# A transformer layer on one core: the last batch's feed-forward part by token halves, and the order of the last three batches

## The chip, the cores and the metric

One core of a Trainium2 chip. The metric is the device time of one execution in microseconds (us). The times of before are those of three runs. A profiled execution has its own time, and a span: from its first to its last instruction. Engines: PE is TensorE, ACT ScalarE, DVE VectorE, POOL GpSimd, and SP issues DMAs.

## What is computed

Eight batches of 1024 tokens of width 128, fp32. Each goes through one attention head and a feed-forward part (FFN) with a layer norm behind either.

```python
q, k, v = x @ wq, x @ wk, x @ wv           # 128 x 128 weights; rotary turn on half of q and k
p = softmax(q @ k.T / 128 + causal mask)
x = layernorm(x + (p @ v) @ wo)            # over the 128 features, no gain or bias
h = gelu(x @ sign(w1).T * alpha1 + b1)     # 512 hidden
x = layernorm(x + h @ sign(w2).T * alpha2 + b2)
```

## The kernel before

Every engine has its own program: a list of small tasks in an order written out by hand, and semaphores between the lists. An engine runs its list strictly in order, so a task that waits holds all that stand behind it. Tasks are named by a number and a batch: `scores(r, c)` is row tile r (128 queries) of batch c; `(h, c)` is half h (512 tokens) of a batch. Batches are 0 to 7, written `B - 1` for 7 and `B - 2` for 6. The text below writes `up(3, 6)` for `up(3, B - 2)`.

One batch goes through these tasks. `x_squares` (DVE) turns x; `xT_high` (ACT) and `xT_low` (POOL) split it into two parts that TensorE's fast format holds. `project` (PE) makes q and k; `rotate` (DVE), `tok_copy` (ACT) and `rotation_sum` (POOL) turn them; `turn_qk` (PE), `qkT_high` (ACT), `qkT_low` (DVE) transpose and split. `scores` (PE), `row_max` (DVE), `exponentials` (ACT), `turn_row` (DVE) and `carry` (SP: 16 DMAs) lead to the transposed probabilities; rows 4 to 7 of the last batch go by `turn_row` on PE and `row_copy` on ACT and DVE instead. `weigh` and `project_out` (PE, with `pxT_copy` on ACT) give the attention output of a half, `residual1` and `statistics1` (DVE), `first_factors` (POOL) and `first_norm` (DVE) the first layer norm.

The FFN: `turn_x1` (PE), `x1T_high` (ACT), `x1T_low` (DVE); `up(j, c)` (PE) makes a quarter j of the hidden features for all 1024 tokens in a PSUM pair of banks; `gelu` and `hidden_high` (ACT) and `hidden_low` (POOL) work on 128 x 1024; `down` (PE) sums the quarters of one half of the tokens; `y_half` (ACT), `turn_y` (PE), `residual2` and `statistics2` (DVE), `second_factors` (POOL), `second_norm` (ACT), `store` (SP).

PSUM holds three pairs of banks and two single banks, given out in rotation (`next_pair`, `next_bank`). A task on PE that takes one waits until the last user of it has been read out (`wait_freed`).

In the last batch of the kernel before, gelu writes back into its PSUM pair for j > 0, and DVE does `hidden_low` for j > 0. `norm_factors` on POOL is a chain of eight small operations per half or batch, the last of them the power -0.5; the second norm has one more, a product. `second_factors` of batch c waits for `s_y`, which the last `second_norm` of batch c - 1 raises. `residual2(0, c)` waits for the `store` of batch c - 2. ACT's Exp and Gelu need a table each, and a change between them puts an ACT_TABLE_LOAD in its queue; its copies need none.

Of the kernel before, what the change touches and what calls it, by code (L numbers as in the profile page):

```python
# [12 lines left out]
LN_EPS = 1e-5  # L13
# [3 lines left out]
def attention_ffn_kernel(nc, x, wq, wk, wv, wo, w1, b1, w2, b2, cos_t, sin_t, out):  # L17
# [32 lines left out]
    with ctx:  # L50
# [123 lines left out]
        def _(sp):  # L174
# [94 lines left out]
        def _(pool):  # L269
# [50 lines left out]
            def shifts(ts, before):  # L320

                norm_factors(stat2, ln2, ts, s_ln2, before, -1.0)
                pool.wait_ge(s_ln2, before + LN_STEPS)
                pool.tensor_tensor(ln2[:, 6, ts], ln2[:, 2, ts], ln2[:, 7, ts], ALU.mult).then_inc(s_ln2, 1)  # L324

            def second_factors(c):
                pool.wait_ge(s_stat2[0], c + 1)
                pool.wait_ge(s_stat2[1], c + 1)
                if c > 0:
                    pool.wait_ge(s_y, c)  # L330
                shifts(slice(0, NT), LN2_STEPS * c)

            def second_factors_half(h, c):
                pool.wait_ge(s_stat2[h], c + 1)
                if h == 0:
                    pool.wait_ge(s_y, c)
                shifts(slice(TG * h, TG * (h + 1)), LN2_STEPS * (c + h))
# [62 lines left out]
            rotation_sum(0, B - 1)  # L400
            rotation_sum(1, B - 1)
            hidden_low(0, 3)
            hidden_low(1, 3)
            hidden_low(2, 3)
            hidden_low(3, 3)
            second_factors(2)
# [8 lines left out]
            first_factors(1, B - 2)  # L415
# [3 lines left out]
            hidden_low(3, B - 3)  # L419
            second_factors(B - 4)  # L420
            first_factors(0, B - 1)
            first_factors(1, B - 1)
# [3 lines left out]
            hidden_low(3, B - 2)  # L426
            second_factors(B - 3)
            hidden_low(0, B - 1)
            second_factors(B - 2)
            second_factors_half(0, B - 1)  # L430
            second_factors_half(1, B - 1)

        @block.tensor
        def _(pe):
# [10 lines left out]
            def wait_freed(task, i, c):  # L445
# [5 lines left out]
                if task == "up":  # L451
                    pe.wait_ge(s_gelu[i], c + 1)
                    if c == LAST and i > 0:
                        pe.wait_ge(s_hid_lo[i], c + 1)
# [146 lines left out]

            def down_quarter(j, h, c):
# [3 lines left out]
                pe.wait_ge(s_hid_lo[j], c + 1)  # L606
# [147 lines left out]
            def ending():  # L754
# [12 lines left out]
                turn_qk(2, B - 2)  # L767
                scores(0, B - 2)
                turn_y(0, 2)
                project(0, B - 1)  # L770
                down(1, 2)
                turn_qk(3, B - 2)
                project(1, B - 1)
                scores(1, B - 2)
                weigh(0, B - 3)
                weigh(1, B - 3)
                weigh(2, B - 3)
                weigh(3, B - 3)
                turn_x1(0, B - 4)
                scores(2, B - 2)  # L780
                scores(3, B - 2)
                turn_y(1, 2)
                project_out(0, B - 3)
                scores(4, B - 2)
                turn_qk(0, B - 1)
                scores(5, B - 2)
                scores(6, B - 2)
                scores(7, B - 2)
                weigh(4, B - 3)
                weigh(5, B - 3)  # L790
                weigh(6, B - 3)
                turn_x1(1, B - 4)
                weigh(7, B - 3)
                up(0, B - 4)
                project_out(1, B - 3)
                down(0, 3)
                down(1, 3)
                up(1, B - 4)
                turn_y(0, 3)
# [9 lines left out]
                scores(1, B - 1)  # L809
                weigh(3, B - 2)  # L810
                turn_y(1, 3)
                scores(2, B - 1)
                scores(3, B - 1)
                project_out(0, B - 2)
                scores(4, B - 1)
                scores(5, B - 1)
                weigh(4, B - 2)
                weigh(5, B - 2)
                weigh(6, B - 2)
                weigh(7, B - 2)  # L820
                turn_x1(0, B - 3)
                scores(6, B - 1)
                scores(7, B - 1)
                turn_x1(1, B - 3)
                down(0, B - 4)
                turn_row(4, B - 1)
                project_out(1, B - 2)
                turn_row(5, B - 1)
                down(1, B - 4)
                up(0, B - 3)  # L830
                up(1, B - 3)
                turn_y(0, B - 4)
                turn_y(1, B - 4)
                up(2, B - 3)
# [451 lines left out]
        def _(dve):  # L1286
# [667 lines left out]
```

## Time and profile before

| | |
|---|---|
| median of 3 runs | 306.39 us (305.84 to 307.79) |
| the profiled execution's own time | 308.83 us |
| its span | 307.0 us |
| granted TensorE clock, mean of the span | 0.962 of full |
| busy: PE, DVE, ACT, POOL | 87%, 75%, 76%, 57% of the span |

The span in 40 slices shows PE at nine tenths or more almost without a break from the eleventh slice to the 33rd, and thin in the last seven. Busy shares are of a whole span, so they say little about the end; the sections below go by stretches of it. In rows of the timeline the first two columns are start and length in us. Rows that stand for several instructions have "xN" and the length of the run. The length of one instruction includes its latency; instructions behind each other overlap, so the pitch (start to start) is shorter. What stands in brackets is the idle time ahead of the row and what ended it. In a row of the windows each engine has its busy time and the number of its instructions, then come the granted clock (1.00 is 2.4 GHz), the DMA share and GB/s.

### The profile page before, as it was taken

To read this page: it belongs to the slowest core of one execution; us is meant where nothing else is said; L and a number is where in the kernel's file an instruction comes from. 1 tells how busy PE (TensorE), PEld (TensorE's weight loads), DVE (VectorE), ACT (ScalarE), POOL (GpSimd) and SP (SyncE) were. 2 spreads that over 40 slices of the span, in tenths; PEclk is the share of its full clock that TensorE was granted. 3 is DMA by queue.
4 is the path that set the end of the run, shared out by engine and by line. 5 is a ranking of instruction groups with operands and counts; after the bars stand their busy time and mean duration, and the time that the engine had idled before them with its cause. 6 is when DMAs were issued, how large, how long until landed. Compare 5 with 4: busy or idle time off the path is not lost.

```text
span 307.0 us, 5699 instructions
## 1 busy us (share of the span) xinstructions
PE 267.2 (87%) x1797; PEld 234.6 (76%) x1797; DVE 230.6 (75%) x551; ACT 233.7 (76%) x385; POOL 175.8 (57%) x281
## 2 busy tenths in 40 slices
PE   0759779999998999999999999999999998959540
PEld 0649578887987898989898989898998897847320
DVE  2399999898988897799779977996696473550832
ACT  1246466555679979998899999887996996897852
POOL 1333424024366396639972884949279769796534
PEclk9969999999999999999999999999999999987985
DMA  9928286377539627652674157114932302002222
GB/s 154 226 64 147 61 135 153 80 111 163 155 74 176 158 52 112 150 136 50 108 166 126 46 138 173 24 46 123 268 83 66 88 2 72 0 0 68 63 71 74
DMA packets 62925, 31.97 MB, mean 104 GB/s; under 512 B 37808, under 2 KB 58800, under 8 KB 62896
## 3 DMA queue, kind: packets, MB, share of 16 engines
q1 hardware_dynamic: 60816, 31.35, 46.2%
q10 hardware_dynamic: 2080, 0.26, 0.6%
q8 instruction: 15, 0.25, 0.3%
q14 instruction: 14, 0.11, 0.1%
HBM read 10.23 MB, written 4.19 MB: 47 GB/s over the span
## 4 chain that ended last, share of the span: by engine, by line
PE 65%; SPq 12%; ACT 8%; DVE 4%; issue 4%; DMA 3%; POOL 2%; ACTq 0%; POOLq 0%; DVEq 0%
PE bank L530 17%; PE pair L510 12%; SPq L212 10%; PE bank L590 4%; PE pair L559 4%; PE bank L591 4%; PE pair L560 4%; PE bank L541 4%; DMA xq<-in_L_attn_x_dram 3%; PE bank L582 3%; ACT res L964 2%; PE pair L572 2%; PE bank L617 2%; PE bank L548 2%; PE pair L574 2%
## 5 line engine op out<-in xcount | busy, mean ns | idle before, releaser
L343 POOL TENSOR_TENSOR hid_lo<-hid,hid_hi 128x1024 fp32r<-128x1024 f32 x29 | 68.5, 2380 | 34.4 <-ACT hid_hi L949 34.4
L530 PE MATMUL bank<-probT,xa 128*128 128x128 f32 x576 | 68.6, 276 | 0.2 <-DMA probT<-turned 0.2
L530 PEld LDWEIGHTS bank<-probT,xa 128*128 128x128 f32 x576 | 66.4, 192 | 0.9 <-DMA probT<-turned 0.3
L902 ACT ACTIVATE prob<-pair,negmax 128x128 f32<-128x128 f32 (+3 forms) x64 | 47.3, 740 | 12.6 <-DVE negmax L1331 10.8
L1331 DVE TENSOR_REDUCE negmax<-pair 128x1 f32<-128x128 f32 (+3 forms) x64 | 47.2, 743 | 6.5 <-PE pair L513 6.3
L1341 DVE STREAM_TRANSPOSE turned<-prob 128x128 f32<-128x128 f32 (+7 forms) x60 | 43.0, 739 | 1.0 <-DMA probT<-turned 1.0
L510 PE MATMUL pair<-qkT_hi 128*128 128x512 f32 (+2 forms) x96 | 37.9, 395 | 3.3 <-ACT tok L916 2.0
L941 ACT ACTIVATE hid<-pair,b_sb,alpha 128x1024 f32<-128x1024 f32 x29 | 34.2, 1203 | 0.8 <-PE pair L560 0.6
L510 PE MATMUL pair<-qkT_hi,qkT_lo 128*128 128x512 f32 (+2 forms) x96 | 33.5, 349 | 0.0
L510 PE MATMUL pair<-qkT_lo,qkT_hi 128*128 128x512 f32 (+2 forms) x96 | 33.4, 348 | 0.0
L313 POOL TENSOR_TENSOR tok<-rot_cos,rot_sin 128x512 f32<-128x512 f32 x16 | 21.1, 1322 | 20.5 <-ACT tok L916 20.5
L964 ACT ACTIVATE res<-res,ln 128x128 f32<-128x128 f32 x60 | 25.9, 489 | 7.7 <-POOL ln L324 7.7
L307 POOL TENSOR_TENSOR xT_lo<-xT,xT_hi 128x512 fp32r<-128x512 f32 x16 | 20.5, 1284 | 19.5 <-ACT xT_hi L909 19.5
L301 POOL TENSOR_TENSOR ln<-ln,minus_half 128x4 f32<-128x4 f32 (+1 forms) x25 | 30.3, 1213 | 2.0
L559 PE MATMUL pair<-x1T_hi,sgn1T 128*128 128x512 f32 x64 | 28.5, 445 | 2.7 <-issue 1.9
L949 ACT ACTIVATE hid_hi<-hid 128x1024 fp32r<-128x1024 f32 x29 | 30.4, 1058 | 0.1
L289 POOL TENSOR_TENSOR ln<-stat 128x4 f32<-128x4 f32 (+1 forms) x25 | 5.1, 206 | 43.7 <-DVE stat L1364 37.6
L1452 DVE TENSOR_TENSOR qkT_lo<-bank,qkT_hi 128x512 fp32r<-128x512 f32 x32 | 21.6, 680 | 8.6 <-ACT qkT_hi L930 8.3
L916 ACT ACTIVATE tok<-pair 128x1024 f32<-128x1024 f32 x16 | 16.4, 1024 | 14.3 <-DVE rot_sin L1447 14.3
L560 PE MATMUL pair<-x1T_lo,sgn1T 128*128 128x512 f32 x64 | 26.9, 420 | 0.0
L1359 DVE SCALAR_TENSOR_TENSOR res<-bank,rinv,xa 128x128 f32<-128x128 f32 x64 | 18.3, 342 | 9.2 <-issue 9.1
L582 PE MATMUL bank<-ident,tok 128*128 128x128 f32 x128 | 20.0, 286 | 5.0 <-DVE qkT_lo L1452 2.7
(97 smaller groups left out, 631.1 us busy)
## 6 DMA issues: line engine op xcount, KB each, us to landing
probT<-turned SPq DMA_DIRECT2D x112, 104.0 KB, 2.2
probT<-turned SPq DMA_DIRECT2D x128, 40.0 KB, 1.9
xa<-in_L_attn_x_dram SPq DMA_DIRECT2D x8, 512.0 KB, 4.5
xq<-in_L_attn_x_dram SPq DMA_DIRECT2D x30, 128.0 KB, 3.8
out_dram<-res SPq DMA_DIRECT2D x7, 512.0 KB, 3.5
cos_sb<-in_cos_dram SPq DMA_DIRECT2D x1, 512.0 KB, 4.5
sin_sb<-in_sin_dram SPq DMA_DIRECT2D x1, 512.0 KB, 6.0
hid<-in_L_ffn_w_dram SPq DMA_DIRECT2D x2, 256.0 KB, 5.2
```

The source lines that it names most:

```text
L212: sp.dma_start(probT[g][k * BLK:(k + 1) * BLK, n, :, :], turned[g][n * BLK:(n + 1) * BLK, k, :, :]).then_inc(s_probT_in[g], 16)
L343: pool.tensor_tensor(hid_lo[:, j, :], hid[:, j, :], hid_hi[:, j, :].bitcast(F32), ALU.subtract).then_inc(s_hid_lo[j], 1)
L510: ins = pe.matmul(dst[:, lo:hi], qp[:, 0, me], kp[:, 1, lo:hi], start=n == 0, stop=n == 2 and not diagonal)
L530: ins = pe.matmul(bank_of["px", r // TG, c][:, me], xa[c % 2][:, j, :], probT[g][:, :, spot + j, :], start=j == 0, stop=j == r)
L559: pe.matmul(dst[:, half(h)], sgn1T[:, j, :], x1T_hi[:, half(h)], start=True, stop=False)
L560: ins = pe.matmul(dst[:, half(h)], sgn1T[:, j, :], x1T_lo[:, half(h)], start=False, stop=True)
L902: act.activation(prob[r % 3][:, 0:(r + 1) * P], pair_of["score", r, c][:, 0:(r + 1) * P], ACT.Exp, bias=negmax[:, r:r + 1], accum_out=rows ...
L941: act.activation(dst, pair_of["up", j, c][:, :], ACT.Gelu, bias=b1_sb[:, j:j + 1], scale=alpha1[:, j:j + 1]).then_inc(s_gelu[j], 1)
L949: act.activation(hid_hi[:, j, :], src, ACT.Copy).then_inc(s_hid_hi[j], 1)
L964: ins = act.activation(res2[c % 2][:, t, :], res2[c % 2][:, t, :], ACT.Identity, bias=ln2[:, 6, t:t + 1], scale=ln2[:, 7, t:t + 1])
L1331: dve.tensor_reduce(negmax[:, r:r + 1], pair_of["score", r, c][:, 0:(r + 1) * P], axis=AX.X, op=ALU.max, negate=True).then_inc(s_max[r], 1)
L1341: dve.transpose(turned[g][:, :, spot:spot + r + 1, :].rearrange("p k m j -> p m k j"), prob[r % 3][:, 0:(r + 1) * P].rearrange("p (m k j) ...
```

## The change

1. Last batch, FFN by halves of the tokens. `up_half(h, q, 7)` makes two quarters of the hidden features for one half in a pair. `gelu_half` works in PSUM (128 x 512, in place) on ACT; `hidden_high_half` is on ACT for j = 0, 2, 3 and on DVE for j = 1; all `hidden_low_half` are on DVE, reading PSUM. `down_quarter` takes all four quarters of the first half and then those of the second.
2. Last batch, both norms: DVE makes mean and variance (`bn_aggr`) and two small operations (`first_means`, `second_means`), POOL the power (and for the second norm the product).
3. All five lists have a new order from about `turn_qk(2, 6)` on. Among the moves: on PE the FFN of batch 5 and its `project_out(1, 6)` stand ahead of `scores(5..7, 7)`, and `up(0..3, 6)` among `weigh(4..7, 7)`; on ACT `gelu(0..3, 5)` ahead of `exponentials(5..7, 7)`; on SP `tokens(6)` ahead of `carry(0, 6)`, and `carry(1, 6)` ahead of `tokens(7)`.

```diff
 # SP
             carry(1, B - 3)
+            tokens(B - 2)
             carry(0, B - 2)
             store(1)
-            tokens(B - 2)
+            carry(1, B - 2)
             tokens(B - 1)
-            carry(1, B - 2)
             carry(0, B - 1)
...
 # POOL
+            def first_rstd(h, c):
+                ts = slice(TG * h, TG * (h + 1))
+                pool.wait_ge(s_ln1[h], LN_STEPS * c + 3)
+                pool.tensor_tensor(ln1[:, 7, ts], ln1[:, 5, ts], minus_half[:, ts], ALU.pow).then_inc(s_ln1[h], 1)
+
+            def second_rstd(h, c):
+                ts = slice(TG * h, TG * (h + 1))
+                before = LN2_STEPS * c + 5 * h
+                pool.wait_ge(s_ln2, before + 3)
+                pool.tensor_tensor(ln2[:, 7, ts], ln2[:, 5, ts], minus_half[:, ts], ALU.pow).then_inc(s_ln2, 1)
+                pool.wait_ge(s_ln2, before + 4)
+                pool.tensor_tensor(ln2[:, 6, ts], ln2[:, 4, ts], ln2[:, 7, ts], ALU.mult).then_inc(s_ln2, 1)
...
             second_factors(B - 4)
-            first_factors(0, B - 1)
-            first_factors(1, B - 1)
+            first_rstd(0, B - 1)
             hidden_low(0, B - 2)
             hidden_low(1, B - 2)
             hidden_low(2, B - 2)
             hidden_low(3, B - 2)
+            first_rstd(1, B - 1)
             second_factors(B - 3)
-            hidden_low(0, B - 1)
             second_factors(B - 2)
-            second_factors_half(0, B - 1)
-            second_factors_half(1, B - 1)
+            second_rstd(0, B - 1)
+            second_rstd(1, B - 1)
 # PE
+            def up_half(h, q, c):
+                pe.wait_ge(s_x1T_lo[h], c + 1)
+                dst = next_pair("up_half", 2 * h + q, c)
+                for k in range(2):
+                    j = 2 * q + k
+                    pe.matmul(dst[:, half(k)], sgn1T[:, j, :], x1T_hi[:, half(h)], start=True, stop=False)
+                    ins = pe.matmul(dst[:, half(k)], sgn1T[:, j, :], x1T_lo[:, half(h)], start=False, stop=True)
+                ins.then_inc(s_up[2 * h + q], 1)
...
+                weigh(6, B - 1)
+                up(3, B - 2)
                 weigh(7, B - 1)
-                project_out(0, B - 1)
+                turn_x1(0, B - 1)
                 project_out(1, B - 1)
-                turn_x1(0, B - 2)
...
+                up_half(0, 0, B - 1)
+                up_half(0, 1, B - 1)
                 turn_y(1, B - 3)
...
                 down(0, B - 2)
                 down(1, B - 2)
+                turn_x1(1, B - 1)
                 turn_y(0, B - 2)
                 turn_y(1, B - 2)
+                up_half(1, 0, B - 1)
+                up_half(1, 1, B - 1)
                 down_quarter(0, 0, B - 1)
+                down_quarter(1, 0, B - 1)
+                down_quarter(2, 0, B - 1)
+                down_quarter(3, 0, B - 1)
                 down_quarter(0, 1, B - 1)
-                down_quarter(1, 0, B - 1)
                 down_quarter(1, 1, B - 1)
-                down_quarter(2, 0, B - 1)
                 down_quarter(2, 1, B - 1)
-                down_quarter(3, 0, B - 1)
                 turn_y(0, B - 1)
                 down_quarter(3, 1, B - 1)
                 turn_y(1, B - 1)
 # ACT
+            def gelu_half(h, j, c):
+                act.wait_ge(s_up[2 * h + j // 2], c + 1)
+                mine = pair_of["up_half", 2 * h + j // 2, c][:, half(j % 2)]
+                act.activation(mine, mine, ACT.Gelu, bias=b1_sb[:, j:j + 1], scale=alpha1[:, j:j + 1]
+                               ).then_inc(s_gelu[j], 1)
...
 # DVE
+            def means(stat, ln, h, done, before):
+                ts = slice(TG * h, TG * (h + 1))
+                for t in tiles(h):
+                    ins = dve.bn_aggr(ln[:, 2:4, t], stat[:, t, :])
+                ins.then_inc(done, 1)
+                dve.wait_ge(done, before + 1)
+                dve.tensor_scalar(ln[:, 4, ts], ln[:, 2, ts], -1.0, None, ALU.mult).then_inc(done, 1)
+                dve.tensor_scalar(ln[:, 5, ts], ln[:, 3, ts], LN_EPS, None, ALU.add).then_inc(done, 1)
...
```

The new end of ACT's list, from `hidden_high(3, 6)` on: `second_norm(0..6, 4)`, `gelu_half(0, 0)`, `(0, 1)`, `(0, 2)`, `second_norm(7, 4)`, `y_half(0, 6)`, `gelu_half(0, 3)`, `hidden_high_half(0, 0)`, `x1T_high(1, 7)`, `y_half(1, 6)`, `hidden_high_half(0, 2)`, `(0, 3)`, `second_norm(0..4, 5)`, `gelu_half(1, 0)`, `second_norm(5..7, 5)`, `gelu_half(1, 1)`, `hidden_high_half(1, 0)`, `gelu_half(1, 2)`, `(1, 3)`, `hidden_high_half(1, 2)`, `(1, 3)`, `y_half(0, 7)`, `second_norm(0..3, 6)`, `y_half(1, 7)`, `second_norm(4..7, 6)`, `second_norm(0, 1, 4, 5; 7)`.

The new end of DVE's list, from `first_norm(0..3, 7)` on: `x1T_low(0, 7)`, `residual1` and `statistics1` of tiles 4 to 7, `first_means(1, 7)`, `residual2(1, 5)`, `statistics2(1, 5)`, `first_norm(4..7, 7)`, `x1T_low(1, 7)`, `hidden_high_half(0, 1)`, `residual2(0, 6)`, `residual2(1, 6)`, `hidden_low_half(0, 0)`, `(0, 1)`, `statistics2(0, 6)`, `(1, 6)`, `hidden_low_half(0, 2)`, `(0, 3)`, `hidden_high_half(1, 1)`, `hidden_low_half(1, 0..3)`, `residual2(0, 7)`, `statistics2(0, 7)`, `residual2(1, 7)`, `second_means(0, 7)`, `statistics2(1, 7)`, `second_means(1, 7)`, `second_norm(2, 3, 6, 7; 7)`.

## Rows read from the trace of the kernel before

**Rows 1.** Windows: 184.5 to 258.5, to 281.6, to the end, all engines.

```profile
184.50:258.50 74.00, 74.00 (x538) 66.98 (x536) 53.21 (x147) 64.90 (x109) 51.53 (x79) 1.00 0.36 90
258.50:281.60 23.10, 18.51 (x77) 14.48 (x77) 10.57 (x35) 19.58 (x26) 19.59 (x34) 0.85 0.16 46
281.60:307.00 25.40, 10.20 (x45) 6.70 (x43) 11.79 (x28) 14.12 (x28) 11.12 (x30) 0.81 0.22 63
```

**Rows 2.** Timeline of PE, 255 us to the end.

```profile
271.58 0.66 PE L548 MATMUL bank<-ident,x 128*128 128x128 f32 x4 [1.60 <-DVE x L1373]
274.08 0.77 PE L559 MATMUL pair<-x1T_hi,sgn1T 128*128 128x512 f32 x1 [1.85 <-issue]
...
297.53 1.08 PE L617 MATMUL bank<-ident,yT 128*128 128x128 f32 x4 [1.50 <-ACT yT L955]
```

**Rows 3.** The chain that ended last, from 200 us: PE's pieces at their pitch.

```profile
216.94 0.44 PE bank L582 x4
...
256.64 1.85 PE bank L541 x16
...
264.93 0.23 PE pair L559
...
274.85 0.43 PE pair L560
```

**Rows 4.** Timeline of ACT, from 187 us.

```profile
187.87 1.28 ACT L902 ACT_TABLE_LOAD   x1
189.16 0.37 ACT L902 ACTIVATE prob<-pair,negmax 128x128 f32<-128x128 f32 x1
...
260.60 0.60 ACT L934 ACTIVATE x1T_hi<-bank 128x512 fp32r<-128x512 f32 x1 [0.44 <-PE bank L548]
...
268.11 2.28 ACT L941 ACTIVATE hid<-pair,b_sb,alpha 128x1024 f32<-128x1024 f32 x2
...
286.24 2.79 ACT L964 ACTIVATE res<-res,ln 128x128 f32<-128x128 f32 x7
...
294.03 0.76 ACT L955 ACTIVATE yT<-bank,b_sb,alpha 128x512 f32<-128x512 f32 x1
...
303.39 0.88 ACT L964 ACTIVATE res<-res,ln 128x128 f32<-128x128 f32 x2 [2.25 <-POOL ln L324]
```

**Rows 5.** Timeline of DVE, from 252 us.

```profile
252.60 0.23 DVE L1350 RECIPROCAL rinv<-rowsum 128x4 f32<-128x4 f32 x2
257.63 2.16 DVE L1359 SCALAR_TENSOR_TENSOR res<-bank,rinv,xa 128x128 f32<-128x128 f32 x8 [4.80 <-issue]
...
270.33 1.19 DVE L1373 TENSOR_SCALAR x<-res,ln 128x128 f32<-128x128 f32 x4
...
273.29 0.69 DVE L1409 TENSOR_TENSOR x1T_lo<-bank,x1T_hi 128x512 fp32r<-128x512 f32 x1 [0.74 <-ACT x1T_hi L934]
...
289.97 2.36 DVE L1396 TENSOR_TENSOR hid_lo<-pair,hid_hi 128x1024 fp32r<-128x1024 f32 x2 [0.20 <-ACT hid_hi L949]
...
296.33 0.87 DVE L1425 BATCH_NORM_STATS2 stat<-res 128x6 f32<-128x128 f32 x4
```

**Rows 6.** Timeline of POOL, from 271 us.

```profile
271.42 7.02 POOL L343 TENSOR_TENSOR hid_lo<-hid,hid_hi 128x1024 fp32r<-128x1024 f32 x3 [0.75 <-ACT hid_hi L949]
278.39 0.21 POOL L289 TENSOR_TENSOR ln<-stat 128x8 f32<-128x8 f32 x1
...
281.82 0.20 POOL L324 TENSOR_TENSOR ln<-ln 128x8 f32<-128x8 f32 x1
...
297.28 0.21 POOL L289 TENSOR_TENSOR ln<-stat 128x4 f32<-128x4 f32 x1 [4.45 <-DVE stat L1425]
...
298.92 1.04 POOL L301 TENSOR_TENSOR ln<-ln,minus_half 128x4 f32<-128x4 f32 x1
```

**Rows 7.** SP's timeline, and DMA issues with KB and median us to landing.

```profile
181.13 30.06 SPq L212 DMA_DIRECT2D probT<-turned  x32
...
out_dram<-res SPq DMA_DIRECT2D x7, 512.0 KB, 3.5
```

More of the change, by code:

```diff
@@ L452, in wait_freed @@
                     pe.wait_ge(s_gelu[i], c + 1)
-                    if c == LAST and i > 0:
-                        pe.wait_ge(s_hid_lo[i], c + 1)
+                if task == "up_half":
+                    h, q = divmod(i, 2)
+                    for j in (2 * q, 2 * q + 1):
+                        pe.wait_ge(s_hid_lo[j], c + 1 + h)
                 if task == "rowT":
@@ L803, in ending @@
                 up(3, B - 4)
+                down(1, 3)
+                turn_y(0, 3)
                 scores(0, B - 1)
-                turn_qk(3, B - 1)
+                scores(1, B - 1)
+                turn_y(1, 3)
+                scores(2, B - 1)
                 weigh(0, B - 2)
@@ L1748, in _ @@
             residual1(7, B - 4)
-            qkT_low(2, B - 2)
-            residual2(0, 2)
-            first_norm(0, B - 4)
             statistics1(4, B - 4)
@@ L1760, in _ @@
-            statistics1(7, B - 4)
+            turn_row(0, B - 2)
             rotate(1, B - 1)
-            reciprocals(1, B - 3)
-            qkT_low(3, B - 2)
-            row_max(1, B - 2)
-            turn_row(0, B - 2)
+            residual2(1, 2)
             statistics2(0, 2)
-            x1T_low(0, B - 4)
-            row_max(2, B - 2)
-            residual2(1, 2)
-            turn_row(1, B - 2)
+            row_max(3, B - 2)
+            first_norm(4, B - 4)
             residual1(0, B - 3)
@@ L1772, in _ @@
             residual1(1, B - 3)
-            row_max(3, B - 2)
-            row_max(4, B - 2)
-            statistics1(0, B - 3)
+            residual1(2, B - 3)
+            first_norm(5, B - 4)
+            turn_row(1, B - 2)
+            first_norm(6, B - 4)
+            first_norm(7, B - 4)
+            residual1(3, B - 3)
+            x1T_low(0, B - 4)
             turn_row(2, B - 2)
             turn_row(3, B - 2)
+            row_max(4, B - 2)
+            x1T_low(1, B - 4)
+            statistics1(0, B - 3)
@@ L1778, in _ @@
+            turn_row(4, B - 2)
+            statistics2(1, 2)
+            statistics1(1, B - 3)
             row_max(5, B - 2)
-            residual1(2, B - 3)
-            residual1(3, B - 3)
             row_max(6, B - 2)
-            first_norm(4, B - 4)
-            turn_row(4, B - 2)
-            statistics1(1, B - 3)
             statistics1(2, B - 3)
-            reciprocals(0, B - 2)
-            first_norm(5, B - 4)
-            first_norm(6, B - 4)
-            first_norm(7, B - 4)
+            row_max(7, B - 2)
@@ L1790, in _ @@
+            turn_row(5, B - 2)
             statistics1(3, B - 3)
+            turn_row(6, B - 2)
             qkT_low(0, B - 1)
-            statistics2(1, 2)
-            turn_row(5, B - 2)
-            x1T_low(1, B - 4)
-            row_max(7, B - 2)
-            turn_row(6, B - 2)
+            turn_row(7, B - 2)
             residual1(4, B - 3)
@@ L1858, in _ @@
             first_norm(3, B - 2)
-            residual2(1, B - 4)
+            statistics1(7, B - 2)
+            residual1(0, B - 1)
+            residual1(1, B - 1)
+            residual1(2, B - 1)
+            residual1(3, B - 1)
+            statistics1(0, B - 1)
+            statistics1(1, B - 1)
+            statistics2(1, B - 4)
             first_norm(4, B - 2)
@@ L1892, in _ @@
             first_norm(3, B - 1)
+            x1T_low(0, B - 1)
+            residual1(4, B - 1)
+            statistics1(4, B - 1)
+            residual1(5, B - 1)
+            residual1(6, B - 1)
+            residual1(7, B - 1)
+            statistics1(5, B - 1)
+            statistics1(6, B - 1)
+            statistics1(7, B - 1)
+            first_means(1, B - 1)
             residual2(1, B - 3)
-            statistics2(0, B - 3)
             statistics2(1, B - 3)
```

425 lines of the change are left out of this document (217 added, 208 removed).

## The prediction

> **What bounds the kernel now.** I read the page's 40 slices first, then the windows around the end, then PE's timeline and the chain, and last the lists of ACT, DVE and POOL beside it. The windows show two regimes. From 184.5, where the new order begins, to 258.5 PE is busy for all of 74.00 us at full clock, with ACT at 64.90 and the others lower [rows 1]: PE's work is the bound. At 258.5 it has just finished `project_out(1, 7)`. From there PE holds 18.51 of 23.10 us and then 10.20 of 25.40, at a granted clock of 0.85 and 0.81 [rows 1]: latency is the bound. What the reader is to see is how little PE work that second regime has. At full clock a 512-column matmul has a pitch of 0.23, a group of four transposes 0.44 and a `project_out` half of 1.85, so 0.93 [rows 3]. Behind 258.5 stand, per FFN batch, 16 of `up` and 16 of `down` (7.5 us) and four groups of transposes (1.8 us); two batches lack all, batch 5 its `down` and `turn_y` (4.6 us). Sum: 2 x 9.2 + 4.6 = 23.0 us. PE could be through at 281.6; it ends at 298.6 [rows 2]. Those 17 us are pauses of 1.60 and 1.85 us and more, and a stretch at half clock, where the pitch is 0.43 [rows 2, 3]. Behind them come the last norm and the store.
>
> **The new order up to the last `weigh`.** I set out each engine's new list from 184.5, gave every task its pitch from the rows, and moved a task back wherever a wait of it ended later. On PE the same sum as above puts the end of all its work at 281.6, and 15.2 us of it stand behind `weigh(7, 7)`: `turn_x1(0, 7)` 0.44, `project_out` 0.93, four `up_half` 3.7, `down(·, 6)` 3.7, `turn_y(1, 5)` and `turn_x1(1, 7)` 0.9, `turn_y(·, 6)` 0.9, eight quarters 3.7, `turn_y(·, 7)` 0.9. So `weigh(7, 7)` can end at 266.4. Against this stand the waits. ACT is close behind: it changes between Exp and Gelu twice more than before (gelu of batch 5 is put inside the exponentials of batch 7), at 1.28 us a load [rows 4], 2.6 us together, and in my walk it hardly rests from 233 us on. I find PE held for about 0.4 us, by `y_half(0, 5)` at 253 and `x1T_low(1, 6)` at 256.7, and margins of only 0.1 to 0.5 us at `turn_qk(2, 7)`, `scores(7, 7)` (waits for `gelu(3, 5)`), `turn_row(4, 7)` (for `exponentials(5, 7)`) and `down(0, 5)` (for POOL's fourth `hidden_low`, 2.3 us each [rows 6]). DVE is held from 233 to 241 by `residual1(4, 6)`, since `project_out(1, 6)` now comes late; queued behind it are `row_max(5..7, 7)`, but their scores are later still, so it costs nothing while PE is full. SP: `tokens(6)` waits for a residual of about 184 and costs `carry(0, 6)` nothing; `carry(0, 7)` is issued from 230 to 240 and is needed at 245 (two carries, 32 DMAs, take SP 30.06 us [rows 7], of which some 10 a carry is issue and the rest waiting for turned rows). I take `weigh(7, 7)` to end at 266.7.
>
> The Trainium skill, ScalarE: Activation LUTs, section What ACT_TABLE_LOAD costs, adds a drain of about 1.4 us to every load; by it the two new changes would take 5.3 us of ACT and the end would come 2.7 us later than below. The trace does not agree: an Exp starts 1.29 us after the start of the load ahead of it, 187.87 to 189.16 [rows 4].
>
> **From the last `weigh` to the last norm.** Prices: 512-wide copy on ACT 0.60, `y_half` 0.76, `second_norm` 0.385 each (2.79 for seven) [rows 4]; 512-wide DVE step out of PSUM 0.69 (pitch 0.60, half of 2.36 / 2 fits), statistics 0.87 for four, `first_norm` 1.19 for four, `residual1` 2.16 for eight [rows 5]. `gelu_half` is not in the trace: between 0.57 (a quarter of 2.28 [rows 4]) and `y_half`'s 0.76; I take 0.65, pitch. `bn_aggr` is not either: its nearest rows are a 128 x 4 reciprocal, 0.23 for two, and the statistics, 0.87 for four [rows 5]; with two small operations and one wait I bound `means` by 0.5 and 1.3 us and take 0.9, for it resembles the small one in elements. It replaces POOL's 1.64 us of small steps (297.28 to 298.92 [rows 6]). The power stays at 1.04.
>
> The walk: `pxT_copy` and `project_out` to 268.3; DVE's residuals and statistics of the second half (queued behind `x1T_low(0, 7)`, 268.6) to 270.6, means to 271.5; POOL has four `hidden_low` of batch 6 first and makes the power to 272.6; `residual2` and `statistics2` of batch 5, then `first_norm` to 274.1. PE meanwhile makes `up_half(0, ·)` and `down(·, 6)` to 274.8, `turn_x1(1, 7)` to 275.2. ACT and DVE split it to 276.8. `turn_y(0, 6)` needs the bank that `y_half(1, 6)` empties, 276.8; `up_half(1, 0)` ends at 278.8. `residual2(0, 6)` waits for `store(4)`, which is released by `second_norm(7, 4)` at 274.0, now behind three `gelu_half`, and lands 3.5 us after its issue [rows 7], near 278. Behind this wait on DVE are the two `residual2`, then `hidden_low_half(0, 0)` and `(0, 1)`, to 280.5, and the pair for `up_half(1, 1)` comes free only then: 281.7. ACT has `second_norm` of batch 5 and the second half's gelu and copies to 285.0, DVE the second half's `hidden_low_half` to 286.3. `y_half(0, 7)` to 285.8, `turn_y(0, 7)`, last quarter to 287.0. ACT is then in `second_norm(0..3, 6)`, which POOL's factors (3.6 us, 278.39 to 282.02 in the old trace [rows 6], here from 282.1) release at 285.7, so `y_half(1, 7)` ends at 288.1, `residual2(1, 7)` at 289.5. `second_means(0, 7)` waits for `second_norm(7, 6)`, 289.6; statistics and second means to 292.3; power and product 1.3; four norms 0.88: 294.5. I add 0.05 us for each of some 25 hand-overs, 1.3 us (a first matmul after a wait takes longer than its pitch, 0.77 against 0.43 [rows 2, 3]): 295.8. In the old trace the last norms end at 304.27 (303.39 + 0.88 [rows 4]) and the span 2.7 us later, which is the last store. New span 298.5, 8.5 less than 307.0. The profiled execution's own time was 2.4 us above the median of the runs; I take the same 8.5 off the median: 306.4 - 8.5 = 298 (297.9).
>
> Work that is priced at nothing: POOL's lost `hidden_low(0, 7)` (2.3 us, it was waited for at 288.9 but POOL is no longer on the path there), and DVE's eight smaller steps for it (of the 23.1 us to 281.6 DVE fills 10.57 [rows 1], which hides most of them; the cover is gone from 280 on, and there they are counted).
>
> **Rivals.** (a) The clock. In before it was at half from 274.08 on, after the two pauses of 1.60 and 1.85 us [rows 2]; a mean of 0.85 over 23.1 us is some 7 us of it [rows 1]. The new walk has pauses of 1.6 us at 275.2 and of 1.7 at 278.8. If the clock falls there, eight matmuls of `up_half` (0.2 us each), two `turn_y` (0.44 each) and the end's share of 0.9 add 3.4 us: 301.3. For it: two pauses as long as those. Against: from 281.6 to the end PE paused for 15.2 of 25.4 us, and the mean grant was still 0.81 [rows 1]. The Trainium skill, TensorE: Matmul & The Clock Gate, section What's actually happening, says that the throttled state is the default and activity lifts it; by that the fuller PE of 258 to 275 keeps its clock, and the trace agrees so far that all of 184.5 to 258.5 ran at 1.00. (b) The narrow margins ahead of 266.7 do not hold. ACT is nearly full there, so a delay of it goes on to everything: each margin missed costs 0.5 to 1.5 us, four or five of them 3 to 6: 301 to 304. (c) The pauses are only moved: the tail's 17 us turn up before the last `weigh`, as DVE's order (`residual1(4, 6)` ahead of `row_max(5..7, 7)`, 8 us of standing still) starves ACT of exponentials. All 8 us would be lost, time 306; against it, the scores it would hold are computed after. (d) Slower: the clock falls at the first pause behind `weigh(7, 7)` and is not lifted again. PE's 15.2 us then cost 0.43 / 0.23 as much, 13 us more, time 311. It decides from about three quarters of that stretch at half clock. In before half clock lasted some 7 us and ended under steady work. (e) The halves do nothing: the end hangs on ACT's backlog of `second_norm(·, 6)`, and the whole gain is the order's. The time is then that of the forecast, within 1.5 us.
>
> **How the numbers follow.** Forecast, with (e) in it: 298, own range 295.5 to 300.5, chance 0.56. (a) 0.17; (b) 0.16; (c) 0.06; (d) 0.05. The low end of the range: both means at 0.5 (0.8 us), `store(4)` not waited for (0.7), no added hand-over time (1.3), 3 us together: 295. The high end takes in (a) and all but the worst of (b): 304. One per cent of 306.4 is 3.1 us, about what a measurement tells from no change: faster is below 303.3. From the cases: faster 0.84 (forecast, (a), two thirds of (b)), same 0.10, slower 0.06.
>
> **What would show it.** PE full and at clock 1.00 to about 266 with `weigh(7, 7)` (last L530-like matmuls) ending there and not at 256.6; two more table loads of 1.28 us on ACT; ACT's busy share above 90% from 235 to 285; `residual2(0, 6)` released by a DMA; `bn_aggr` at 0.06 to 0.2 us; last power starting less than 1 us behind the last statistics. It is wrong if PE has pauses of over 1 us before 266, or if the second half's gelu starts after 283.

## The result and the profile after

The changed kernel takes 299.12 us (median of 4 runs, 297.07 to 299.45), the kernel before 306.78 on the same chip (4 runs, 305.84 to 307.79): ratio 0.9727, 95% interval 0.9693 to 0.9761. The profiled execution took 299.45, its span is 296.6. The spans of the two profiles differ by 10.4 us, the medians by 7.7. The profiled execution of before was 2 us above its median, so what is read below as the difference between the two profiles is 2 to 3 us too large over the whole span, and the verdicts of the experiments rest on ratios of times.

Windows of after, over the first two stretches of [rows 1] and then to its end:

```profile
184.50:258.50 74.00, 73.91 (x516) 66.16 (x515) 55.95 (x156) 69.44 (x115) 54.22 (x84) 1.00 0.38 95
258.50:281.60 23.10, 19.86 (x119) 16.39 (x117) 13.72 (x49) 22.66 (x39) 14.85 (x18) 1.00 0.08 23
281.60:296.60 15.00, 4.64 (x20) 2.59 (x20) 8.86 (x32) 8.78 (x19) 5.13 (x10) 0.76 0.35 105
```

PE is as full as before up to 258.5. Behind it PE is busy for 24.5 us where it was 28.7 [rows 1], though its work is nearly the same: most of that is the half clock which is gone (0.85 before, 1.00 now, in the middle stretch). Its idle time fell from 19.8 to 13.6. ACT went from 64.90 to 69.44 and from 19.58 to 22.66 of 23.10: it is the second full engine.

PE's timeline of after: the end of `weigh(7, 7)`, and every pause of over half a microsecond behind it. [rows 2] has three pauses of before.

```profile
264.00 1.95 PE L536 MATMUL bank<-probT,xa 128*128 128x128 f32 x16
...
276.19 1.06 PE L633 MATMUL bank<-ident,yT 128*128 128x128 f32 x8 [1.61 <-ACT yT L981]
...
279.49 0.47 PE L614 MATMUL pair<-x1T_hi,sgn1T 128*128 128x512 f32 x1 [1.29 <-DVE hid_lo L1429]
...
283.43 0.47 PE L623 MATMUL bank<-hid_hi,sgn2T 128*128 128x512 f32 x1 [0.56 <-DVE hid_lo L1429]
...
287.23 0.63 PE L633 MATMUL bank<-ident,yT 128*128 128x128 f32 x4 [1.06 <-ACT yT L981]
```

Before's longest pause is not in [rows 2]. It is needed below, for the clock: behind it PE ran on at 1.00 (the windows of 287 to 289 and of 289 to 291 us, and the pitch is 0.23).

```profile
288.91 0.47 PE L607 MATMUL bank<-hid_hi,sgn2T 128*128 128x512 f32 x1 [2.75 <-POOL hid_lo L343]
289.22 0.39 PE L608 MATMUL bank<-hid_lo,sgn2T 128*128 128x512 f32 x1
289.45 0.40 PE L607 MATMUL bank<-hid_hi,sgn2T 128*128 128x512 f32 x1
```

ACT's timeline of after. The first row lies ahead of the new order and serves as a fixed point: from there to the start of the last norms it is 113.67 us.

```profile
179.25 1.28 ACT L956 ACT_TABLE_LOAD   x1
...
270.60 2.07 ACT L968 ACTIVATE pair<-pair,b_sb,alpha 128x512 f32<-128x512 f32 x3
...
284.09 0.79 ACT L981 ACTIVATE yT<-bank,b_sb,alpha 128x512 f32<-128x512 f32 x1
...
286.30 0.79 ACT L981 ACTIVATE yT<-bank,b_sb,alpha 128x512 f32<-128x512 f32 x1
...
290.77 0.88 ACT L990 ACTIVATE res<-res,ln 128x128 f32<-128x128 f32 x2 [2.14 <-POOL ln L342]
292.92 0.88 ACT L990 ACTIVATE res<-res,ln 128x128 f32<-128x128 f32 x2 [1.27 <-POOL ln L342]
```

DVE's and POOL's timelines of after. Read the first DVE row with the first POOL row: DVE's four `first_norm` of the half (0, 7) end at 260.38, and POOL starts `hidden_low` of batch 6 at 260.25, under the last of them.

```profile
259.30 1.08 DVE L1406 TENSOR_SCALAR x<-res,ln 128x128 f32<-128x128 f32 x4
...
276.86 1.29 DVE L1474 TENSOR_TENSOR res<-bank,x 128x512 f32<-128x512 f32 x2 [0.16 <-PE bank L633]
...
288.71 0.38 DVE L1436 BATCH_NORM_AGGREGATE ln<-stat 128x2 f32<-128x6 f32 x4
...
290.84 0.38 DVE L1436 BATCH_NORM_AGGREGATE ln<-stat 128x2 f32<-128x6 f32 x4 [0.69 <-POOL ln L342]
```

```profile
260.25 7.02 POOL L348 TENSOR_TENSOR hid_lo<-hid,hid_hi 128x1024 fp32r<-128x1024 f32 x3 [1.10 <-ACT hid_hi L963]
...
289.45 1.01 POOL L340 TENSOR_TENSOR ln<-ln,minus_half 128x4 f32<-128x4 f32 x1 [4.79 <-DVE ln L1440]
```

### The profile page after: what moved, and what is told of

The parts are those of the page before. It is cut to its first block, busy times and chain, and to the rows that moved or that the text cites. A ratio compares the mean times of both kernels' runs of the same rounds, so it can differ in the third digit from the quotient of the medians.

```text
span 296.6 us, 5713 instructions
## 1 busy us (share of the span) xinstructions
PE 264.4 (89%) x1797; PEld 233.4 (79%) x1797; DVE 235.0 (79%) x581; ACT 236.4 (80%) x394; POOL 167.8 (57%) x252
## 4 chain that ended last, share of the span: by engine, by line
PE 74%; ACT 11%; DVE 7%; issue 2%; DMA 2%; POOL 1%; SPq 0%; ACTq 0%; POOLq 0%; DVEq 0%
PE bank L536 21%; PE pair L516 17%; PE bank L547 5%; PE bank L588 4%; PE bank L596 4%; PE pair L565 4%; PE bank L597 4%; PE pair L566 4%; ACT res L990 3%; PE bank L554 2%; PE pair L578 2%; PE pair L580 2%; PE pair L579 2%; DMA xq<-in_L_attn_x_dram 2%; PE bank L633 2%
## 5 line engine op out<-in xcount | busy, mean ns | idle before, releaser
L348 POOL TENSOR_TENSOR hid_lo<-hid,hid_hi 128x1024 fp32r<-128x1024 f32 x28 | 66.3, 2383 | 31.3 <-ACT hid_hi L963 31.2
L516 PE MATMUL pair<-qkT_hi 128*128 128x512 f32 (+2 forms) x96 | 38.6, 402 | 2.9 <-ACT tok L932 1.9
L956 ACT ACTIVATE hid<-pair,b_sb,alpha 128x1024 f32<-128x1024 f32 x28 | 32.9, 1203 | 0.1
L963 ACT ACTIVATE hid_hi<-hid 128x1024 fp32r<-128x1024 f32 x28 | 29.3, 1057 | 0.5 <-PE bank L597 0.4
L301 POOL TENSOR_TENSOR ln<-ln,minus_half 128x4 f32<-128x4 f32 (+1 forms) x21 | 26.2, 1247 | 1.6
L289 POOL TENSOR_TENSOR ln<-stat 128x4 f32<-128x4 f32 (+1 forms) x21 | 4.4, 208 | 39.3 <-DVE stat L1397 29.7
L565 PE MATMUL pair<-x1T_hi,sgn1T 128*128 128x512 f32 x56 | 23.6, 421 | 0.9 <-ACT prob L918 0.9
L946 ACT ACTIVATE qkT_hi<-bank 128x512 fp32r<-128x512 f32 x32 | 18.7, 596 | 6.4 <-PE bank L588 6.4
```

What stands on the lines that cost most here:

```text
L301: pool.tensor_tensor(rstd, part, minus_half[:, ts], ALU.pow).then_inc(done, 1)
L348: pool.tensor_tensor(hid_lo[:, j, :], hid[:, j, :], hid_hi[:, j, :].bitcast(F32), ALU.subtract).then_inc(s_hid_lo[j], 1)
L516: ins = pe.matmul(dst[:, lo:hi], qp[:, 0, me], kp[:, 1, lo:hi], start=n == 0, stop=n == 2 and not diagonal)
L565: pe.matmul(dst[:, half(h)], sgn1T[:, j, :], x1T_hi[:, half(h)], start=True, stop=False)
L956: act.activation(hid[:, j, :], pair_of["up", j, c][:, :], ACT.Gelu, bias=b1_sb[:, j:j + 1], scale=alpha1[:, j:j + 1]).then_inc(s_gelu[j], 1)
L963: act.activation(hid_hi[:, j, :], hid[:, j, :], ACT.Copy).then_inc(s_hid_hi[j], 1)
```

## The experiments

Twelve kernels on three chips, e1 to e4, e5 to e8 and e9 to e12. Each ratio is to the kernel before on the same chip (medians there: 307.32, 308.14 and 308.46 us). After was not run again beside them, so a comparison with it assumes that a ratio carries over from chip to chip. Where a difference of two ratios is also given in us, it is that share of 306.8. The last column is the stretch from the fixed point to the start of the last norms, in the one execution that was profiled; in before it is 123.56, in after 113.67.

In three profiles this stretch has something that no edit made: the table load near 233 us comes 53.10 or 53.11 us behind the fixed point in after and in seven of the others that have the new order, but 54.01 in e1 and e9 and 53.51 in e2, ahead of all that those edits change. PE's timeline of e9 shows what it was waiting for, a DMA of the probabilities (e1 has the same wait of 0.71, e2 one of 0.22, and the other profiles with the new order none):

```profile
226.66 2.72 PE L536 MATMUL bank<-probT,xa 128*128 128x128 f32 x22 [0.71 <-DMA probT<-turned]
```

So 0.9 us of the stretches of e1 and e9 and 0.4 of e2's are not the edit's.

| | kernel | median, us | ratio, interval | stretch |
|---|---|---|---|---|
| | after | 299.12 | 0.9727 (0.9693 to 0.9761) | 113.67 |
| e1 | after without the means | 302.91 | 0.9863 (0.9834 to 0.9892) | 119.83 |
| e2 | after without the halves | 306.26 | 0.9973 (0.9953 to 0.9993) | 121.43 |
| e3 | order alone | 310.32 | 1.0108 (1.0080 to 1.0136) | 124.55 |
| e4 | before and the means | 306.16 | 0.9968 (0.9948 to 0.9988) | 121.46 |
| e5 | e1, POOL held back | 302.95 | 0.9827 (0.9790 to 0.9864) | 117.63 |
| e6 | e2, PE's pause filled | 303.82 | 0.9873 (0.9840 to 0.9906) | 118.34 |
| e7 | halves and means, old order | 306.40 | 0.9937 (0.9907 to 0.9966) | 121.19 |
| e8 | after, ACT + 2.1 us | 301.75 | 0.9788 (0.9750 to 0.9826) | 115.73 |
| e9 | after, PE + 1.87 us | 300.67 | 0.9744 (0.9711 to 0.9776) | 116.09 |
| e10 | after, own tile for `ln2` | 298.09 | 0.9669 (0.9637 to 0.9701) | 112.43 |
| e11 | after, 8 norms to DVE | 305.56 | 0.9896 (0.9862 to 0.9930) | 119.91 |
| e12 | e10 and e11 | 303.61 | 0.9838 (0.9803 to 0.9872) | 118.53 |

**e1: the means taken back.**

```diff
-            first_rstd(0, B - 1)
+            first_factors(0, B - 1)
...
-            second_rstd(0, B - 1)
+            second_factors_half(0, B - 1)
# DVE: first_means and second_means of both halves left out
```

> The changed kernel (299.1) with both norms of its last batch made on GpSimd as before; halves and order stay. Theory A, each part acts on the path: GpSimd's small steps take 1.64 us against some 0.73 that VectorE's means measured, and in the second norm the second half's chain of 3 us queues behind the first half's, so the last norms start 1.8 us later; with up to 0.9 us from the first norm: 300.9 to 301.8. Rival B, the means only fill time that ACT's backlog costs anyway: 299.1 to 299.6.

The ratio is 1.4% above after's, 4.2 us of 306.8: more than either theory gave the means. The stretch is 6.2 longer, 5.3 without that DMA wait; the execution that was profiled is the slowest of the six. The end gives its share: POOL's chain of two halves stands on the path, one row of 0.20 to 1.04 us after the other from 293.30 to 299.14, where after has a power of 1.01 and a product. From the end of the last statistics to the last norms it is 5.14 us, in after 2.78: 2.4 us. The rest comes from a place that neither theory had named. Timelines of DVE, POOL and PE in e1:

```profile
261.86 7.29 DVE L1418 TENSOR_SCALAR x<-res,ln 128x128 f32<-128x128 f32 x4 [1.47 <-POOL ln L301]
```

```profile
261.80 7.01 POOL L360 TENSOR_TENSOR hid_lo<-hid,hid_hi 128x1024 fp32r<-128x1024 f32 x3
```

```profile
269.20 0.66 PE L566 MATMUL bank<-ident,x 128*128 128x128 f32 x4 [2.25 <-DVE x L1418]
```

Four `first_norm` steps take 7.29 us instead of 1.08. With POOL's eight small steps in place of one power DVE's norms wait 1.47 us for them and then meet POOL's `hidden_low`. Three of the four lasted about as long as one POOL operation (2412 ns at most), the fourth 334 ns (the median of all 64 in the kernel is 340). POOL's own three run at their usual length. PE then waits 2.25 us, and `up_half(0, 0)` starts at half clock. The Trainium skill, SBUF — State Buffer, section Who interferes with whom, has a rule for it: VectorE and GpSimd share one pair of ports, and an instruction that takes it locks the other engine out until it ends. The rows agree.

**e5: e1 with POOL held back until `first_norm(3, 7)` is done.**

```diff
+            pool.wait_ge(s_x1[0], B)
             hidden_low(0, B - 2)
```

> e1 (GpSimd makes both norms of the last batch, 302.9) with one wait more: GpSimd starts hidden_low(0, 6) only when first_norm(0..3, 7) is through. In e1 the four first_norm took 7.29 us, as long as GpSimd's three hidden_low beside them (7.01), against 1.08 in the changed kernel, and TensorE's turn_x1(0, 7) came 3.4 us later. Theory A, VectorE's tensor_scalar and GpSimd's tensor_tensor on SBUF can't run side by side: the four take 1.1 us again, turn_x1(0, 7) follows at once and the end comes 1 to 3 us sooner: 300 to 302. Rival B, the long first_norm has another cause, or the second half sets the end anyway: 302.9 or, with GpSimd 1 us later, 303.5.

```profile
261.65 1.12 DVE L1419 TENSOR_SCALAR x<-res,ln 128x128 f32<-128x128 f32 x4 [1.46 <-POOL ln L301]
```

```profile
262.85 9.38 POOL L360 TENSOR_TENSOR hid_lo<-hid,hid_hi 128x1024 fp32r<-128x1024 f32 x4 [1.23 <-DVE x L1419]
272.19 0.21 POOL L289 TENSOR_TENSOR ln<-stat 128x4 f32<-128x4 f32 x1
```

DVE's timeline has the norms back at 1.12 us, so the collision is shown to be what made them long. The time hardly follows: 0.9827 to e1's 0.9863 is 1.1 us, with intervals that overlap, the low edge of theory A at best. POOL, now later, starts the factors of the second half at 272.19, `first_norm(4, 7)` waits for them, and half clock comes in `up_half(1, ·)` instead, 279.80 to 283.6.

**e2 and e6: the FFN by whole quarters, then with PE's pause filled.**

```diff
-                up_half(0, 0, B - 1)
-                up_half(0, 1, B - 1)
...
+                up(0, B - 1)
+                up(1, B - 1)
+                up(2, B - 1)
+                up(3, B - 1)
# gelu, hidden_high and hidden_low as in before
# e6, ahead of the first down_quarter, all overwritten by it:
+                    for _ in range(16):
+                        pe.matmul(dst[:, :], sgn1T[:, 0, :], x1T_hi[:, half(0)], start=True, stop=True)
```

> The changed kernel with the last batch's FFN made by whole quarters of all 1024 tokens as before (its up stands where the second half's stood, GpSimd has hidden_low(0) again); means and order stay. Theory A: up of 3.7 us can only begin with the second half's x1T at 277, and gelu, copies and differences of twice the width follow it; my walk has the last norms 2 us later: 301 to 302. Rival B (case e of the prediction), the end hangs on ACT's backlog of second norms and the halves do nothing: within 0.5 of 299.1. Rival C, the halves are most of the gain: 304 or more.

> e2 (whole FFN, 306.3) with 16 matmuls of 512 columns more, whose result is overwritten, put in TensorE's 4.5 us pause ahead of down_quarter(0, 0). In e2 the seven quarters behind that pause ran at a pitch of 0.43 (285.97 to 291.65). Theory A, the clock falls for the pause and that costs the end 2 to 3 us: quarters at 0.23, 303.3 to 304.5. Rival B, the clock is low there for another reason, or ACT sets the end: 306 to 307.

PE's timeline of e2, then of e6:

```profile
285.97 0.76 PE L626 MATMUL bank<-hid_hi,sgn2T 128*128 128x512 f32 x1 [4.50 <-POOL hid_lo L348]
286.53 0.63 PE L627 MATMUL bank<-hid_lo,sgn2T 128*128 128x512 f32 x1
286.96 0.63 PE L626 MATMUL bank<-hid_hi,sgn2T 128*128 128x512 f32 x1
```

```profile
279.17 3.90 PE L627 MATMUL bank<-x1T_hi,sgn1T 128*128 128x512 f32 x16
283.79 0.50 PE L629 MATMUL bank<-hid_hi,sgn2T 128*128 128x512 f32 x1 [0.73 <-POOL hid_lo L348]
284.13 0.40 PE L630 MATMUL bank<-hid_lo,sgn2T 128*128 128x512 f32 x1
284.36 0.40 PE L629 MATMUL bank<-hid_hi,sgn2T 128*128 128x512 f32 x1
```

Without the halves 2.5% are lost (7.5 us), nearly the whole gain: rival C. A quarter for all 1024 tokens has a copy of 1.04 us and, for the first quarter, POOL's 2.34 us between gelu and `down`, and PE stands still for 4.50 us. Behind that its pitch is 0.43, half clock, through seven of the eight quarters. e6 keeps PE at work through the pause; the pitch is 0.23 and 1.0% (3.1 us) comes back, as its theory A has it. So of the 7.5 us that the halves are worth some 3 are clock, and the remaining 4.4 are put down to the shorter latency; no run takes those apart.

**e3, e4, e7: the parts alone.** e3 is after with the edits of e1 and e2; e4 is before with the means; e7 is before's order with halves and means:

```diff
# e7, PE: before's list, with
-                up(0..3, B - 1)
+                up_half(0, 0, B - 1)
+                up_half(0, 1, B - 1)
+                up_half(1, 0, B - 1)
+                up_half(1, 1, B - 1)
# and gelu_half, hidden_*_half and means in the places of what they replace
```

> The changed kernel with both other parts undone: only the new order of the five lists is left. Theory A, the parts add up: 303 to 304, so the order is worth 3 to 4 of the 7.7 us. Rival B, the order is all of it: 299 to 300. Rival C, the order only pays with the halves: 306 or more.

> The kernel before (306.8) with the means alone: VectorE makes mean and variance of the last batch's two norms, GpSimd the powers; order and whole FFN stay. Theory A: the second norm's last chain is on the path there too (GpSimd's steps from 300.33 to 302.04 after the statistics at 300.25), 1 to 1.8 us less: 305 to 305.8. Rival B: nothing, 306.8.

> The old order of all five lists with both other parts of the change: the last batch's FFN by halves (up_half(0, .), down(., 6), up_half(1, .), quarters by halves, ACT's and VectorE's list ends as in the changed kernel) and the means. The order alone was 3 us slower than before (e3). Theory A, the order pays only under the halves: down(., 6) ends 6 to 7 us later here than in the changed kernel, and what follows it is the same: 304 to 306. Rival B, the order costs as much here as alone: 295 to 297. Rival C, it does nothing: 299.

The order alone costs 1.1% (3.3 us), rival C: it moves batch 7's latency chain to where POOL is in `hidden_low` (its DVE row is 7.29 us again, at 262.07) and leaves whole quarters at the end. The means alone bring 0.3% (1.0 us, the low edge of theory A), halves and means without the order 0.6% (theory A); these two intervals overlap, so halves alone are not shown to help there. With all three it is 2.7%. Given the other two, the order is worth 2.1%, the halves 2.5%, the means 1.4%: 6.0% together, more than twice the gain. The traces show one reason: the order brings `first_norm` next to POOL's `hidden_low`, and the means keep the two apart (e1, e5). Why halves and order need each other is argued and was not taken apart.

**e8 and e9: which engine binds up to 266.**

```diff
# e8, ACT, ahead of exponentials(5, 7)
+            for n in range(2):
+                act.wait_ge(s_spare, n)
+                act.activation(spare[:, :], cos_sb..., ACT.Copy).then_inc(s_spare, 1)   # 128 x 1024
# e9, PE, up(2, 5) and up(3, 5)
-                for h in range(NG):
+                for h in range(NG) if c != B - 3 or j < 2 else (0, 1, 0, 1):
```

> The changed kernel (299.1) with two copies of 128 x 1024 more on ACT (2.1 us, into a spare tile that nothing reads) ahead of exponentials(5, 7) at about 233 us. Theory A, ACT is as full as TensorE from there on (1 to 1.3 us idle to 266): the end comes 1 to 2 us later, 300 to 301.2. Rival B, only TensorE sets the pace ahead of 266: at most 0.3 us.

> The changed kernel with the first product of batch 5's last two quarters made twice: eight more 512-column matmuls, at 0.23 us each 1.87 us of TensorE ahead of scores(5,7), into the same bank with the same accumulate flags order (hid of these quarters is not the reference's). Theory A (TensorE is a bound of the stretch to 266 as much as ScalarE is; e8 showed 2.1 us of ScalarE work costing 1.9): everything from there is later by 1 to 1.9 us, ratio to the kernel before 0.979 to 0.982, about 300.3 us. Rival B (only ScalarE bounds, TensorE has slack between its waits for it): at most 0.5 us, ratio 0.973 to 0.975.

(In e9 the second pair of products starts its sums anew, so `hid` is unchanged, other than the expectation says.) e8: 2.1 us of ACT cost 0.6%, 1.9 us, and 2.06 in the stretch: ACT binds. e9's two measures disagree. By the ratio PE's 1.87 us cost 0.5 us, rival B; in the profile the stretch is 2.42 longer, of which 0.91 is the DMA wait and 1.5 the edit's, theory A. ACT shows where it enters:

```profile
179.81 1.28 ACT L956 ACT_TABLE_LOAD   x1
...
233.82 1.28 ACT L956 ACT_TABLE_LOAD   x1
...
259.55 1.28 ACT L956 ACT_TABLE_LOAD   x1
...
295.90 0.88 ACT L990 ACTIVATE res<-res,ln 128x128 f32<-128x128 f32 x2 [1.27 <-POOL ln L342]
```

The load of 259.55 is 79.74 behind the fixed point, in after it is 77.33 (256.58): 2.41, and at the load of 233.82, ahead of the added matmuls, it was 0.91 already. On the same chip e9 is 2.6 us slower than e10, whose gain over after is 1.2 to 1.8, which leaves 0.8 to 1.4. So the profile says that PE binds too; by the ratio e9 can't be told from after (0.9711 to 0.9776 against 0.9693 to 0.9761), and whether the 1.87 us cost 0.5 or 1.5 stays open.

**e10: the last batch's second-norm statistics in a tile of their own.**

```diff
+        ln2z = sb("ln2z", [P, LN_STEPS, NT])
...
-                if h == 0:
-                    dve.wait_ge(s_y, c)
...
-                means(stat2, ln2, h, s_ln2, before)
+                means(stat2, ln2z, h, s_ln2, before)
...
-            residual2(1, B - 1)
             second_means(0, B - 1)
+            residual2(1, B - 1)
```

> The changed kernel with a tile of its own for the last batch's second-norm statistics, so that the first half's means need not wait for second_norm(7,6), and with those means ahead of residual2(1,7) on VectorE. In the changed kernel's trace that half's means start at 288.71, when ScalarE's norm ends, and the second half's means wait for GpSimd's first half (0.69 us), so the last norms start at 292.92. Theory A: the first half's powers start near 286.5 and end before the second half's means are ready, so the end is earlier by 0.9 to 1.5 us: ratio 0.968 to 0.970, about 297.9 us. Rival B: ScalarE's first four norms of the last batch take over as the thing that ends last (each 0.44 us, after the norms of batch 6), or residual2(1,7) is late behind the means: less than 0.4 us, ratio 0.972 to 0.973.

ACT's timeline of e10, and DVE's:

```profile
179.93 1.28 ACT L957 ACT_TABLE_LOAD   x1
...
290.14 0.88 ACT L991 ACTIVATE res<-res,ln2z 128x128 f32<-128x128 f32 x2 [0.80 <-POOL ln2z L343]
292.36 0.88 ACT L991 ACTIVATE res<-res,ln2z 128x128 f32<-128x128 f32 x2 [1.34 <-POOL ln2z L343]
```

```profile
287.17 0.87 DVE L1482 BATCH_NORM_STATS2 stat<-res 128x6 f32<-128x128 f32 x4
288.08 0.38 DVE L1437 BATCH_NORM_AGGREGATE ln2z<-stat 128x2 f32<-128x6 f32 x4
```

Theory A holds for the end: the stretch is 1.24 shorter. The means now start right behind the statistics, where in after they stood 1.4 us longer; the first power comes 1.3 us earlier and not the 2.9 that the expectation gave it. 0.9669 is the best ratio of all. Against the kernel before it is clear of the noise; against after it is 0.6% with intervals that overlap a little, so the profile's 1.24 us is the better evidence.

**e11 and e12: batch 4's second norms to DVE.**

```diff
# ACT
-            second_norm(0..7, B - 4)
# DVE, behind first_norm(3, 7); e12 has the edits of e10 as well
+            second_norm_all(B - 4)
```

> The changed kernel with batch 4's eight second_norms taken from ScalarE (some 3.1 us near 266 to 270) and made by VectorE behind first_norm(3,7), beside GpSimd's three hidden_low runs of 260.25 to 267.27. Theory A (each of VectorE's tensor_scalar steps can be held for as long as one GpSimd instruction lasts, as e1 showed where four of them took 7.29 us instead of 1.1): eight of them take 5 us or more, x1T_low(0,7) and with it up_half(0,7) come later, and the relief of ScalarE is lost: no gain or a loss, 299 to 302 us, ratio 0.973 to 0.983. Rival B (the steps take 0.27 to 0.35 us each, 2.5 us in the 6.7 us in which VectorE waits for x1T_high(0,7) in any case): ScalarE is free 3 us sooner, and pxT(1,7) and the gelu halves follow: 296.5 to 297.5, ratio 0.965 to 0.968.

> The two edits of e10 and e11 in one kernel. If each does what its own theory gives, the time is e11's less 0.9 to 1.5 us: 297.5 to 301 with a held VectorE, 295 to 296.5 with a free one. If the end is set by ScalarE's norms of batch 6 alone, the two overlap and the sum is no better than the better of them by more than 0.5 us.

```profile
262.37 10.36 DVE L1452 TENSOR_SCALAR res<-res,ln 128x128 f32<-128x128 f32 x8
272.65 0.68 DVE L1466 TENSOR_TENSOR x1T_lo<-bank,x1T_hi 128x512 fp32r<-128x512 f32 x1
```

```profile
262.31 7.03 POOL L348 TENSOR_TENSOR hid_lo<-hid,hid_hi 128x1024 fp32r<-128x1024 f32 x3 [1.09 <-ACT hid_hi L963]
270.15 2.50 POOL L348 TENSOR_TENSOR hid_lo<-hid,hid_hi 128x1024 fp32r<-128x1024 f32 x1 [0.81 <-ACT hid_hi L963]
```

```profile
273.38 0.80 PE L614 MATMUL pair<-x1T_hi,sgn1T 128*128 128x512 f32 x1 [3.47 <-DVE x1T_lo L1466]
```

The three timelines of e11 (DVE, POOL, PE) are e1's collision made on purpose: eight steps in 10.36 us, POOL hardly disturbed, PE idle for 3.47 and then at half clock. The loss of 1.7% (5.2 us) is larger than theory A's 3 us at most; the theory had left out the clock, and how much of the loss is the clock's no run tells. e12 is 0.6% below e11, as e10 is below after: the two edits add.

## Why the prediction was right, and where it was not

The total was 298.0, the time 299.12. Its steps against the profile of after:

| step | predicted | seen |
|---|---|---|
| `weigh(7, 7)` ends | 266.7 | 265.8 (264.00 + 1.95, with latency) |
| `up_half(1, 0)` ends (next start) | 278.8 | 278.0 (277.81 + the pitch) |
| `up_half(1, 1)` starts, ends | 280.5, 281.7 | 279.49, 280.50 |
| `y_half(0, 7)`, `y_half(1, 7)` end | 285.8, 288.1 | 284.88, 287.09 |
| `second_means(0, 7)` starts | 289.6 | 288.71 |
| last norms end | 295.8 | 293.80 |
| span | 298.5 | 296.6 |

Up to `second_means(0, 7)` each step is 0.8 to 1.2 us early, and 0.6 of that was there ahead of 184.5 already: the fixed point stands at 179.25, in before at 179.83. The last norms are 2.0 early, for one reason: the walk itself ended them at 294.5, and the prediction added 1.3 us for hand-overs on top. The trace shows no room for this term, and it is the largest error of the sum. What the profile gave beyond the forecast the median took back: the forecast subtracted 8.5 from the median, and 7.7 were measured. The walk's span is 1.9 us too long and the total 1.1 too short; that the two errors nearly cancel is luck.

**Right.** PE full and at 1.00 to the last `weigh`, ACT behind it (busy 9.57 or more of each 10 us from 230 to 280), two more table loads at 1.28. `residual1(4, 6)` held DVE for 8.3 us ahead of 240.15 and cost nothing. `gelu_half` has a pitch of 0.67 (three take 2.07, one 0.72; 0.65 taken). `second_means(0, 7)` waits for `second_norm(7, 6)`, and e10 shows that this wait and the order behind it cost 1.2 us. `bn_aggr` is 0.09 a tile, inside its sign of 0.06 to 0.2.

**Rival (a), the clock, did not come**, though the pauses did: 1.61 and 1.29 us, and the clock stayed at 1.00 to the end of PE's work. Its price of 3.4 us was not tested; e6 puts half clock over fourteen matmuls of e2's end at some 3 us. The prediction's argument for it, "two pauses as long as those", went by the length of a pause, and the length of one does not decide: in e5 one of 1.14 and one of 1.45 us were followed by half clock, in after one of 1.61 was not, and nor was the 2.75 of before, which its own trace had. What does decide is not shown here.

**Terms that were off.** `store(4)` was not waited for: its issue was at 273.11, and `residual2(0, 6)` at 276.86 was released by PE, where the prediction named a DMA as a sign. It cost little: `hidden_low_half(0, 1)` ends at 279.34, where the walk has 280.5, and the walk is about 0.9 late all along. `means` takes 0.66 (288.71 to the power at 289.45 is 0.74 with the hand-over), not 0.9. The second half's means wait 0.69 us for POOL's product of the first half, a wait that the walk did not have. By it a second sign fails: the last power starts 1.43 us behind the last statistics (290.14 to 291.57) and not less than 1.

**What did not hold is (e)**, which the forecast counted in: "The halves do nothing", and the whole gain is the order's. e3 has the order alone at 3.3 us slower, e2 has the halves at 7.5 us. The mechanism that (e) named, ACT's backlog of `second_norm(·, 6)`, exists, as the wait ahead of `second_means(0, 7)`; but e10 prices it at 1.2 us, and it does not make the halves worthless. The walk's sum had all three parts in it and so came out right; the credit for each did not.

**What the prediction missed** is DVE against POOL. It costed `first_norm` at 1.19 wherever it stood. In after it is 1.08, but narrowly: the last of the four is under way when POOL starts at 260.25. The prediction had no term for this, so that it came out is luck. That the means on DVE shorten POOL's chain ahead of this point, and so keep the two apart, is part of why they are worth 1.4%, 4.2 us, and not the 0.74 that the walk gives each of them (1.64 less 0.9).

## What to carry to other kernels

Parts of a change to a latency chain don't add: test each by taking it out of the whole, not by putting it in alone, or a part that pays only with the others is thrown away. Before work is moved to an engine that looks idle, look at what runs beside it at that time, POOL beside DVE above all: DVE was idle for 6.72 us in after and still had no room for 2.5 us of norms. Where a long pause of PE can't be avoided, try matmuls that nobody reads: here they gave back 3.1 us.

## What the runs showed of the hardware

- DVE's `tensor_scalar` of 128 x 128 out of SBUF, 0.34 us, takes up to 2.43 us beside a GpSimd `tensor_tensor` of 128 x 1024, which keeps its 2.35. Four took 7.29 beside three of them (e1, e3), eight 10.36 beside four (e11). Not all of DVE's work is held: beside POOL's `hidden_low` of 271.52 in e1 three `residual1` (out of PSUM) took 0.85 and three statistics 0.67, their usual lengths.
- Pauses of 1.14 and 1.45 us within 4 us (e5), 2.25 and 0.39 (e1), 3.47 (e11) and 4.50 (e2) were followed by half clock for some 2 to 6 us. Pauses of 1.61 (after), of 2.23, 0.61 and 0.63 (e3), of 2.75 (before, 288.91) and of 3.11 (e3, 290.74) left it at 1.00. Their length alone does not tell which it will be. 16 matmuls in the pause of e2 kept it at full (e6).
- `bn_aggr` for four tiles of 128 x 6 takes 0.38, GpSimd's power of 128 x 4 1.01 to 1.04, of 128 x 8 1.67.
